# The start of a fused cross-attention and mixture-of-experts kernel: the second head's weight product ahead of the transpositions, the exponential table behind the rows' copies, the first query product in parts

## The reference, cut to what matters

```python
x = x + xattn(layernorm(x), ctx_512, ...)      # x: 2 x 256 rows of 256; ctx: 2 x 512 rows of 64
x = x + ffn(layernorm(x), ...)                 # 32 experts, 4 of them per row, and a shared one

def xattn(hidden_q, kv_c, Wq, w_kc_q, w_kc_kv, W_qr, W_kr, Wo):     # 16 heads of 128
    q_hk  = (hidden_q @ Wq.T).reshape(B, S, H, K)
    q_big = einsum('bshk,hkq->bshq', q_hk, w_kc_q)                  # 192 wide for each head
    q_big = apply_rope(q_big, sin_q, cos_q)
    kv_r  = apply_rope(kv_c, sin_k, cos_k)
    q_r   = einsum('bshq,hqr->bhsr', q_big, W_qr)
    k_r   = einsum('bld,hdr->bhlr', kv_r, W_kr)
    attn  = softmax(einsum('bhsr,bhlr->bhsl', q_r, k_r))
    ctx_c = einsum('bhsl,bld->bhsd', attn, kv_r)
    return (einsum('bhsd,hkd->bhsk', ctx_c, w_kc_kv) as rows) @ Wo.T
```

## Time and profile before

| | us |
|---|---|
| median of three runs | 305.81 (305.61 to 305.84) |
| the profiled execution, its own time | 305.71 |
| span of its core in the trace | 303.5 |
| TensorE busy (matmul) | 286.5 (94% of the span) |
| VectorE busy | 182.1 (60%) |
| ScalarE busy | 159.2 (52%) |
| GpSimd busy | 133.9 (44%) |

### The profile page before, as it was taken

The page is one execution under the profiler, slowest core; times in us unless marked ns, Lnnn a source line. Parts: engine busy times, 40 slices in busy tenths (PEclk is TensorE's granted clock), DMA queues, the critical chain, the costliest instruction groups (busy, mean ns, idle before and its releaser), DMA issues.

```text
span 303.5 us, 5498 instructions
## 1 busy us (share of the span) xinstructions
PE 286.5 (94%) x1847; PEld 204.1 (67%) x1847; DVE 182.1 (60%) x432; ACT 159.2 (52%) x378; POOL 133.9 (44%) x124
## 2 busy tenths in 40 slices
PE   7988899999999999999999999988789999999983
PEld 6665767765778675777666877754467666667663
DVE  4595766658776777767575275337862222353576
ACT  3544877686666676786766164377203333342430
POOL 0661937795008591039970000000075555555663
PEclk9999999999999999999999999999999999999998
DMA  7950006200620000700009991602023454433224
GB/s 229 399 215 3 0 1 181 98 0 2 194 85 2 0 3 0 249 13 1 2 14 364 405 402 64 243 2 69 0 84 92 146 162 149 153 107 85 70 79 132
DMA packets 15850, 34.14 MB, mean 113 GB/s; under 512 B 2512, under 2 KB 8400, under 8 KB 15824
## 3 DMA queue, kind: packets, MB, share of 16 engines
q1 hardware_dynamic: 13520, 27.51, 25.3%
q0 software_dynamic: 2304, 6.29, 7.3%
HBM read 30.12 MB, written 3.67 MB: 111 GB/s over the span
## 4 chain that ended last, share of the span: by engine, by line
PE 84%; DVE 8%; DMA 3%; ACT 2%; issue 2%; DVEq 0%; ACTq 0%; POOLq 0%
PE bank L675 10%; PE bank L572 10%; PE bank L555 9%; PE bank L546 6%; PE bank L547 5%; PE bank L526 5%; PE bank L696 4%; PE bank L441 4%; PE bank L443 4%; PE bank L442 4%; PE bank L470 3%; PE bank L664 3%; PE bank L501 3%; PE bank L641 3%; PE bank L504 3%
## 5 line engine op out<-in xcount | busy, mean ns | idle before, releaser
L1341 POOL DMA_INDIRECT rope<-xn_rows,idx x32 | 31.1, 973 | 83.3 <-DVE idx L1236 61.9
L347 POOL TENSOR_TENSOR rtmp<-abuf,rope 128x512 f32<-128x512 f32 x21 | 27.3, 1302 | 60.3 <-PE bank L443 41.0
L842 ACT ACTIVATE prob<-bank,nmax 128x512 f32<-128x512 f32 x48 | 32.7, 685 | 36.7 <-DVE nmax L1026 36.7
L1026 DVE TENSOR_REDUCE nmax<-bank 128x1 f32<-128x512 f32 x64 | 41.1, 684 | 6.5 <-PE bank L547 6.0
L675 PE MATMUL bank<-wall,nmat 128*64 (+1 forms) x256 | 31.2, 385 | 0.8 <-ACT nmat L917 0.8
L572 PE MATMUL bank<-pT,kvr 128*64 128x256 f32 x256 | 31.2, 385 | 0.0
L1044 DVE COPY pT<-bank 128x512 f32<-128x512 f32 x32 | 22.0, 687 | 12.3 <-PE bank L555 12.1
L546 PE MATMUL bank<-kdup,qsp 128*128 128x512 f32 x64 | 28.3, 443 | 0.8 <-ACT prob L842 0.8
L998 DVE COPY abuf<-bank 64x512 f32<-64x512 f32 x24 | 16.4, 684 | 19.4 <-ACT abuf L818 19.1
L350 POOL TENSOR_TENSOR roped<-rtmp 128x512 f32<-128x512 f32 x21 | 27.2, 1295 | 1.6
L348 POOL TENSOR_TENSOR rtmp<-abuf,rope 128x512 f32<-128x512 f32 x21 | 27.4, 1307 | 0.0
(11 more groups left out here) (206 smaller groups left out, 562.1 us busy)
## 6 DMA issues: line engine op xcount, KB each, us to landing
wall<-in_w_exp SPq DMA_DIRECT2D x32, 384.0 KB, 7.3
wring<-in_w_attn SPq DMA_DIRECT2D x16, 224.0 KB, 4.3
wring<-in_w_attn SPq DMA_DIRECT2D x4, 640.0 KB, 8.1
y_rows<-nmat SPq DMA_DIRECT2D x10, 256.0 KB, 2.2
wring<-in_w_attn SPq DMA_DIRECT2D x4, 512.0 KB, 7.0
rope<-in_rope_q SPq DMA_DIRECT2D x1, 768.0 KB, 6.7
x_sb<-in_x SPq DMA_DIRECT2D x1, 512.0 KB, 3.6
xn_rows<-xn SPq DMA_DIRECT2D x4, 128.0 KB, 1.7
```

The costliest lines, as they stand in the source:

```text
L347: eng.tensor_tensor(t0.rearrange("p (b s) -> p b s", b=B), own.rearrange("p (b s) -> p b s", b=B), cos, ALU.mult)
L842: act.activation(probs[t % 4], s_ps[t % 3][:, :], ACT.Exp, bias=nmax[:, t:t + 1], accum_out=psum_e[:, t:t + 1]).then_inc(s_exp, 1)
L1026: dve.tensor_reduce(nmax[:, t:t + 1], s_ps[t % 3][:, :], AX.X, ALU.max, negate=True).then_inc(s_max, 1)
L1341: pool.indirect_dma_start(xg[:, u % XG, :], None, xn_dram, bass.IndirectOffsetOnAxis(idx[:, u:u + 1], 0)) \
```

## The change

The prologue's list is reordered: head 1's weight product, M1, stands directly behind M0 and ahead of X (all three engines that take part in it move it), the fill between M0 and X is one matmul in place of two, and a new step E, ScalarE's alone, holds the dummy Exp, behind X. The first piece of the query product, A0, goes through a new function, `first_turned`, which issues the same six passes in another order and waits for the parts that each needs, where before all six waited for the whole of `xT_lo`.

```diff
-        PROLOGUE = [... "W6 M0 W2 X0 M1 W3 A0 B0 x0 G0 C0 M2 W5 z0 M3 R0 K0 R1 R2 A1 B1 C1 G1".split()]
+        PROLOGUE = [... "W6 M0 M1 W1 X0 E0 W3 A0 B0 x0 G0 C0 M2 W5 z0 M3 R0 K0 R1 R2 A1 B1 C1 G1".split()]
...
+            def first_turned(u):
+
+                m_hi, m_low = m_v[:, 0, :, 0, 0, :], m_v[:, 1, :, 0, 0, :]
+                pe.wait_ge(wk_out, use(0, "M", 1) + 1)
+                for dc in range(ND):
+                    pe.wait_ge(xT_hi, dc + 1)
+                    pe.matmul(work[u % 2][:, :], m_hi[:, dc, :], xnT[:, 0, dc, :], start=(dc == 0), stop=False)
+                pe.wait_ge(m_lo, 2)
+                for dc in range(ND):
+                    pe.matmul(work[u % 2][:, :], m_low[:, dc, :], xnT[:, 0, dc, :], start=False, stop=False)
+                for dc in range(ND):
+                    pe.wait_ge(xT_lo, dc + 1)
+                    mm = pe.matmul(work[u % 2][:, :], m_hi[:, dc, :], xnT[:, 1, dc, :], start=False, stop=(dc == ND - 1))
+                mm.then_inc(wk_full, 1)
...
                 elif kind in "ABC":
                     k = "ABC".index(kind)
+                    if u == use(0, "A", 0):
+                        first_turned(u)
+                        return
                     pe.wait_ge(m_lo, HG * g + 2 * i + 2)
-                    if g == 0:
-                        pe.wait_ge(xT_lo, ND)
...
             act.activation(std[:, 0:TT, 0], mv[:, 0:TT, 1], ACT.Sqrt, bias=epsc[:, :]).then_inc(ln_std, 1)
-            act.activation(warm[:, 0:1], epsc[:, :], ACT.Exp)
...
+                elif kind == "E":
+                    act.activation(warm[:, 0:1], epsc[:, :], ACT.Exp)
```

More of the change, by code:

```diff
@@ L299, in steps @@
                 yield (g, s[1], int(s[2])) if s[0] == "-" else (g + 1, s[0], int(s[1]))
-        PROLOGUE = [(0, s[0], int(s[1])) for s in "W6 M0 W2 X0 M1 W3 A0 B0 x0 G0 C0 M2 W5 z0 M3 R0 K0 R1 R2 A1 B1 C1 G1".split()]
+        PROLOGUE = [(0, s[0], int(s[1])) for s in "W6 M0 M1 W1 X0 E0 W3 A0 B0 x0 G0 C0 M2 W5 z0 M3 R0 K0 R1 R2 A1 B1 C1 G1".split()]
         SEQ = PROLOGUE + [s for t in range(TILES) for s in steps(t)]
```

## The result

| | before | changed |
|---|---|---|
| median of 20 runs each, us | 306.10 (305.56 to 307.97) | 305.63 (303.88 to 306.21) |
| ratio, 95% interval | | 0.9964 (0.9946 to 0.9982) |
| the profiled execution, its own time | 305.71 | 305.63 |
| span | 303.5 | 303.4 |

What follows compares the result with a forecast made beforehand. TensorE, busy 94% of the span, was taken as the bound, so its saturated stretch must start earlier: 1.42 us won at A0 and B0, 1.26 kept past the rotations; 305.71 - 1.26 = 304.45, plus 0.10, about 304.6 us (range 304.2 to 305.4).

Steps and rivals of the forecast that it cites:

- TensorE up to X: Prologue: M0 from 5.62, M1 to 7.0, W1 to 7.45; X loses nothing or at most some hundredths of a us.
- The slower rival: Head 1's weights, now ahead of the transpositions, land late and delay X; 307.5 us if landed at 9.6; chance 0.04.
- ScalarE and VectorE: Prologue: table load from about 9.88 to 11.29 hidden by A0; weights' low parts done 9.45, rows' near 10.1 and 10.75.
- A0 and B0: First query products: A0 from 9.90 to 11.38, B0 at 11.38 instead of 12.80; 1.42 us won.
- Where part of it stays: Rotation x0: keys' copy on GpSimd until 14.61 holds VectorE, L347 ends 0.55 later; gain 1.26 instead of 1.42 us.
- the first rival: Rotation x0: the lock leaves it alone and VectorE keeps 1.42 us, giving 304.4 us; chance 0.12.
- From there to the end: After the rotations: everything down the chain, including first scores and the saturated stretch, moves earlier by 1.26 us.
- The spread: Whole kernel: runs lie within 0.23 us, so about 0.2%, or 0.6 us, is what a measurement can tell.
- The number: Whole kernel: 305.71 - 1.26 = 304.45, median of runs 0.10 above, so about 304.6 us; chance 0.64.
- GpSimd goes first: Rotations: y0's first operation takes its turn ahead of x0's, x0 ends at 19.7, gain gone, 305.7 us; chance 0.07.
- The absorbed start: Attention: TensorE waits for something with its own time, gain shrinks to 0.3 us or less, 305.5 us; chance 0.09.

Runs made afterwards that it cites:

- less fill: Changed kernel with four fill matmuls in place of six ahead of M0 and none ahead of X; median 304.64 us, ratio to before 0.9933.
- the second profile of the changed kernel: The changed kernel unedited, run and profiled again against the kernel before; median 305.66 us, ratio 0.9965, span 302.4.
- the longer keys: Changed kernel with one more unused 128x512 copy (0.61 us) on GpSimd behind the keys' last; executed once, L347 ended at 15.76, 0.54 behind the copy.
- one fill matmul behind X: Changed kernel with four fill matmuls ahead of M0, none ahead of X, and one in place of three behind X; median 304.50 us, ratio to before 0.9941.
- the table alone: Kernel before with only the exponential table load moved, behind M1's copies, which stay behind X; ratio to before 1.0007.

## Why the prediction was right, and where it wasn't

**TensorE up to X: wrong by 0.4 us in this execution.** I took M0's start at 5.62 from the one trace as fixed. It hangs on the first fill, which ended 0.37 later here, and since the change puts M1 and W1 between M0 and X, the whole row of them pushed X's transpositions to 7.83 in place of 7.43. Most of that was absorbed, since their end is set by VectorE's last tile (8.21 here, 8.26 before): X's copies came 0.12 later. The slower rival had this place right and its cause wrong. Head 1's weights landed 4.5 us after their issue, at 6.6, and no row of the changed kernel's two profiles shows a wait for them; TensorE's own slow passes pushed X. Only with less fill does TensorE wait for those weights (0.43), and it then costs nothing. The prediction gives 3.95 us for the first twelve passes; that stretch, 1.45 to 5.40, holds only the first eleven, and the twelve took 4.17.

**ScalarE and VectorE: right.** The load lay from 10.00 to 11.29 behind X's copies and hid behind A0. The two low parts of the weights ended at 9.27, the rows' at 10.82 (10.75 forecast). The 1.38 us of drain that the Trainium skill ("ScalarE: Activation LUTs", What ACT_TABLE_LOAD costs) adds to a table load shows in none of the traces: the next instruction follows the load's 1.28 within 0.02, and A0's copy starts 1.59 after the start of the load, which is when A0 is done.

**A0 and B0: right.** 9.82 and 11.39, where 9.90 and 11.38 were worked out; B0's copy at 13.00, 1.40 earlier, where 1.42 was.

**Where part of it stays: the mechanism right, its size off in the first profile.** 1.26 was forecast for x0's end, 1.41 was measured (18.39 against 19.80), which by itself would have fitted the first rival, that the lock leaves x0 alone. The keys' chain had moved after all: their table landed 0.24 earlier in that execution, GpSimd's copy ended at 14.39, and x0, at 14.33, hardly met it. In the second profile of the changed kernel it did. GpSimd and VectorE there:

```profile
13.80 0.61 POOL L1336 COPY kvr<-kvr 128x512 f32<-128x512 f32 x1
```

```profile
14.00 0.95 DVE L347 TENSOR_TENSOR rtmp<-abuf,rope 128x512 f32<-128x512 f32 x1
```

L347 ended at 14.95, 0.54 behind the copy's end at 14.41; the sum had 0.55. That is the step as costed, and the longer keys confirm it. Here the trace agrees with the rule of the Trainium skill ("SBUF — State Buffer", SBUF: two separate sides) that the pair of ports is held for a whole instruction, by whoever starts first.

**From there to the end: right to 215.86, wrong behind it.** "All of it moves" held to 0.02 us through the attention. It stopped in the routing stage, because I read the granted clock of one execution, 1.00 up to the last slice, as the kernel's. Its fall there is an event that most executions of both kernels have in some form: the mean clock was 0.993 or less in 76 of the 93 executions of before in the three later series, and in 20 of the 32 of the changed kernel. What it costs depends on what TensorE has to do at that moment. In the profile after, it took 0.88.

**The spread: wrong.** The prediction took 0.23 us from three runs as the kernel's spread. Twenty runs reach from 305.56 to 307.97.

**The number: partly luck.** That 304.7 meets 304.6 is not the shift of 1.26 arriving whole at the end. Against before's lower group the changed kernel's mean is ahead by 0.4 us only, by 0.5 in its second series (305.58 against 306.04), and what brings the means 1.1 apart is before's upper group, of which the prediction knew nothing. Even without a fall of the clock some is lost on the way: from the first scores to the end of the span it is 271.5 us in both such profiles of the old order, and 271.8 to 272.0 in the three of the new one. Where these 0.3 to 0.5 us go wasn't settled; the three wait 0.15 to 0.40 us for one of the last gathers, and the two don't.

**The rivals.** That GpSimd goes first at 14.61 was seen in none of the traces; the mirror image (VectorE first, the keys' copy between), met with one fill matmul behind X, was worth 0.8 us to the better. The absorbed start came about in one execution, at a place the rival didn't name. What remains open is the kernel before's upper group of executions, 1.6 to 1.9 us above the lower (7 of 20). In the later series all 32 executions with a mean clock of 0.985 to 0.987 belong to it, and six more at 0.991 to 0.993. The profile of the table alone (0.985) is the nearest look at one: the clock was low from 215 to 222 and the rows came 8.28 behind the tables, 1.1 more than before, and its scores had come 0.6 later, with a slow first fill. Together that is about the distance of the groups, but it is one profile, and of an edited kernel. Why the changed kernel's executions at that clock (304.98 to 306.20, seven of 20) don't form such a group was not settled, and 0.6 to 0.7 of the 1.1 us is this difference.

## What to carry to other kernels

When several inputs of one product are made in a chain, look at which pass needs which input: here reordering the makers and splitting the waits won 0.48 us each and 1.52 together, while moving the 1.3 us table load, the longest thing in sight, won nothing in either order of the steps. A start that is 1.4 us earlier passes through a saturated stretch of 185 us unchanged, but one trace doesn't tell what the stages with idle time behind it do, so read two or three of them. And take more than three runs before calling a spread: when a kernel's runs lie in two groups, compare the groups, for a ratio of all runs mixes them. Filler ahead of the critical path should be counted at half speed, where it may run.

## What the runs showed of the hardware that was not expected

- TensorE's first passes after the start run at half speed for a varying time: twelve fill passes took from 4.15 to 5.29 us, against 2.6 at 0.216 us each, while the granted clock of the rows reads 1.00.
- The granted clock fell to 0.50 in the routing stage of nine of the fourteen profiles, behind 2.30 busy us of 4 in the first profile of the changed kernel and 6.34 of 8 in the second; the kernel before had 6.37 of 8, 3.16 of 4 and 2.74 of 4 there and no fall. It began between 212 and 218, and cost 0.9 us where TensorE had back-to-back work, and nothing that shows where it had idle time behind it.
- The order in which GpSimd and VectorE take their turns can be worth more than the overlap itself: in one profile a 0.61 us copy in one turn, in place of a 1.28 us tensor operation, brought the first scores 0.9 us forward. What decided it was the landing of a 256 KB load, after which the keys' work began between 9.1 and 9.7 us.
